# An expert stage worked in pairs of tiles, its first pair prepared inside the attention steps

## What is computed

```python
xn = layernorm(x)
x  = x + attention(xn) + ffn(xn)

def gating(t, sim, gates):                 # one weight per token and expert
    logits = normalize(t) @ normalize(sim) - sigmoid(gates)
    gated  = relu(logits)                  # experts with gated > 0 are active;
    ...                                    # a token with none gets its two best
    return softmax(masked gated)

def ffn(x):
    n1 = layernorm(x, w, b); rw = gating(n1, ...)
    q, k, v = weighted sums over 8 experts; attn = causal softmax attention
    hs = x + weighted sum over 8 experts of attn @ o_proj
    n2 = layernorm(hs, w, b); rw2 = gating(n2, moe_sim, moe_gates)
    inter = gelu(n2 @ w1[e])               # per expert e
    return hs + sum_e rw2[:, e] * (inter @ w2[e])
```

## Time and profile before

| | us |
|---|---|
| median of 3 runs | 1577.72 (1576.56 to 1579.24) |
| profiled execution | 1577.96 |
| its span, first to last instruction | 1576.2 |
| TensorE busy | 1338.6 (85%) |
| VectorE busy | 1081.8 (69%) |
| ScalarE busy | 815.0 (52%) |
| GpSimd busy | 341.4 (22%) |

### The profile page before, as it was taken

How to read it: one execution, slowest core, us unless ns; L and a number is a source line. 1 busy time by engine, 2 the same in 40 slices (tenths; PEclk the granted TensorE clock), 3 DMA queues, 4 the chain that set the end, 5 groups by cost and what they waited for, 6 DMA issues and landing times.

```text
span 1576.2 us, 34759 instructions
## 1 busy us (share of the span) xinstructions
PE 1338.6 (85%) x10534; PEld 1024.4 (65%) x10628; DVE 1081.8 (69%) x4153; ACT 815.0 (52%) x1752; POOL 341.4 (22%) x422
## 2 busy tenths in 40 slices
PE   1289999999899999999999999999994588888887
PEld 0157777777777777777777777777773355555555
DVE  7567766777777667777776777777634577777771
ACT  1136556566655566666556566665662344444342
POOL 3011221111122111111221111112111233333332
PEclk9689999999999999999999999999997699999999
DMA  4413323222233232322333322233200333223332
GB/s 108 96 45 77 79 73 100 74 78 69 68 82 76 76 99 68 79 68 72 80 75 85 89 77 70 69 79 79 75 34 10 115 135 127 102 107 134 133 135 81
DMA packets 86696, 133.21 MB, mean 85 GB/s; under 512 B 9163, under 2 KB 77115, under 8 KB 77371
## 3 DMA queue, kind: packets, MB, share of 16 engines
q1 hardware_dynamic: 86098, 132.10, 29.5%
q10 hardware_dynamic: 488, 0.01, 0.0%
HBM read 108.76 MB, written 21.50 MB: 83 GB/s over the span
## 4 chain that ended last, share of the span: by engine, by line
PE 54%; DVE 18%; ACT 11%; issue 9%; DMA 4%; DVEq 1%; SPq 1%; POOL 1%; ACTq 0%; POOLq 0%
PE ps L1363 6%; PE ps L1364 5%; PE ps L1408 5%; PE ps L1373 5%; PE ps L1572 4%; PE ps L1341 4%; PE ps L1237 3%; DMA qst<-mT 3%; PE ps L1322 3%; ACT pr L651 2%; DVE ats L1164 2%; PE ps L1299 2%; PE ps L1564 2%; PE ps L1292 2%; PE ps L1295 1%
## 5 line engine op out<-in xcount | busy, mean ns | idle before, releaser
L651 ACT ACTIVATE pr<-ps 128x512 f32<-128x512 f32 x384 | 227.2, 592 | 176.6 <-PE ps L1322 155.7
L1007 DVE TENSOR_REDUCE mx<-ps 128x2 f32<-128x512 f32 (+1 forms) x384 | 264.2, 689 | 49.8 <-PE ps L1299 26.8
L515 POOL TENSOR_TENSOR n1s<-rep,n1T 128x256 f32<-128x256 f32 x256 | 176.9, 729 | 292.5 <-PE ps L1373 274.7
L656 ACT ACTIVATE ps<-trn 128x512 f32<-128x512 bf16 x382 | 229.7, 601 | 12.1
L1572 PEld LDWEIGHTS ps<-w2s,ats 128*128 128x128 f32 x1024 | 127.3, 191 | 91.7 <-DVE ats L1164 47.8
L1572 PE MATMUL ps<-w2s,ats 128*128 128x128 f32 x1024 | 140.3, 280 | 34.2 <-DVE ats L1164 26.6
L522 POOL TENSOR_TENSOR zt<-xn,rstd 128x256 f32<-128x256 f32 x32 | 19.6, 612 | 655.2 <-DVE rstd L849 655.2
L1363 PE MATMUL ps<-n1s,wq 128*128 128x256 f32 x512 | 159.8, 394 | 0.0
L783 ACT ACTIVATE n1s<-ps 128x512 f32<-128x512 f32 x128 | 76.4, 597 | 156.5 <-PE ps L1564 155.1
L1364 PE MATMUL ps<-n1s,wk 128*128 128x256 f32 x512 | 152.7, 380 | 0.0
L1373 PE MATMUL ps<-wv,n1s 128*128 128x128 f32 x1024 | 150.6, 280 | 0.0
(11 more groups left out here) (222 smaller groups left out, 2482.2 us busy)
## 6 DMA issues: line engine op xcount, KB each, us to landing
rep<-scr_rw SPq DMA_DIRECT2D x32, 1024.0 KB, 5.1
qst<-scr_rw SPq DMA_DIRECT2D x8, 2048.0 KB, 7.5
kst<-scr_rw SPq DMA_DIRECT2D x8, 2048.0 KB, 7.5
scr_parts<-parts SPq DMA_DIRECT2D x64, 192.0 KB, 2.3
qst<-scr_parts SPq DMA_DIRECT2D x192, 64.0 KB
kst<-scr_parts SPq DMA_DIRECT2D x32, 192.0 KB
xt<-in_x SPq DMA_DIRECT2D x32, 128.0 KB, 2.3
kst<-scr_parts SPq DMA_DIRECT2D x32, 128.0 KB
```

What stands on the lines that cost most here:

```text
L515: pool.tensor_tensor(n1s[:, e], rep[:, par, e], n1T[:, par], ALU.mult).then_inc(n1s_done, 1)
L651: act.activation(pr[:, G % 2, i], ps[:, S2[k % 2]], ACT.Exp).then_inc(exp_done, 1)
L656: act.activation(ps[:, S2[k % 2]], seeds[:, 1 if (k + 2) % 3 == 2 else 0], ACT.Copy).then_inc(seed_done, 1)
L1007: dve.tensor_reduce(mx[:, min(i, 1), h:h + n], ps[:, S1[k % 2]].rearrange("p (h t) -> p h t", h=n), AX_X, ALU.max, negate=True).then_inc(s ...
```

## The change

Tiles are prepared in pairs (`NP` = 8 pairs, `BP` = 8 blocks):

- One `layer_norm2`, one `gating` and one `weights_T2` per pair, on 8 blocks at once. The gating of the next pair lies in the first tile of a pair, beside scalings 2 to 6 (`GELU_AT`), the norm of the pair after that behind it.
- The logits are formed by token: for each block of 128 tokens the normalised block itself is the stationary operand and the 8 columns of `simn` (or 2 columns of ones, for the squared norm) move. There is no copy and no transpose back.
- GpSimd does nothing in this stage. The norm is applied by ScalarE (`scale_norm2`, one instruction per block with scale and bias), all scalings are VectorE's. `n2T` has eight buffers and `hg` four (two of each before), so the copy `place_norm2` is gone, and the pipeline of up, gelu, scaling and down runs on across tiles: `up(k + 2)` follows `down(k)` for k from 0 to 127.
- The weights go to DRAM in eight pieces a pair, and come back in two halves of 1 MB a tile.
- The norm of the first pair is computed in the attention step before the last, that of the second pair, and the logits, gating and weights of the first pair, in the last one.

The diff without its removed lines and without what repeats:

```diff
+LN2_LINKS = 3 + 10
+NP = MS // 2
+BP = 2 * TM
+LG_W = 16
+GELU_AT = (5, 11, 17, 22, 28)
...
+            def store_weights2(g):
                 sp_.wait_ge(rwT2_done, g + 1)
+                for t in (2 * g, 2 * g + 1):
+                    if t >= 4:
+                        sp_.wait_ge(rep2_lo_in[t % 2], 16 * (t // 2 - 1))
+                        sp_.wait_ge(rep2_hi_in[t % 2], 16 * (t // 2 - 1))
+                    r = TM * E * (t % 2)
+                    for i in range(TM):
+                        sp_.dma_start(scr_rw2[t % 4, :, i], rwT[r + E * i:r + E * i + E, 0:P]).then_inc(rw2_stored, 16)
+            def spread2(t):
+                sp_.wait_ge(rw2_stored, 16 * 2 * TM * (t // 2 + 1))
+                for half, arrived in enumerate((rep2_lo_in, rep2_hi_in)):
+                    if t < 2:
+                        sp_.wait_ge(s2_out, UNITS * (NB - 1 + t))
+                    else:
+                        sp_.wait_ge(hgs_done, E * (t - 2) + E // 2 * (half + 1))
+                    src = scr_rw2[t % 4, E // 2 * half:E // 2 * (half + 1)].rearrange("(o e) i p -> o (e i p)", o=1)
+                    sp_.dma_start(rep2[t % 2][half].rearrange("p e t -> p (e t)"),
+                                  src.broadcast_to((P, E // 2 * W2))).then_inc(arrived[t % 2], 16)
...
+            store_weights2(0)
+            spread2(0)
             sp_.wait_ge(base_done, NB)
             store_base(NB - 1, 1)
+            spread2(1)
             sp_.wait_ge(base_stored, 16 * NB)
+            sp_.wait_ge(pv_out, NG * NB)
+            load_base(0)
+            for g in range(NP):
+                if g:
+                    store_out(2 * g - 1)
+                load_base(2 * g + 1)
+                if g + 1 < NP:
+                    store_weights2(g + 1)
+                    spread2(2 * g + 2)
+                store_out(2 * g)
+                if g + 1 < NP:
+                    load_base(2 * g + 2)
+                    spread2(2 * g + 3)
+            store_out(MS - 1)
+            for stored in out_stored:
+                sp_.wait_ge(stored, 16 * NP)
...
+            def scale_norm2(t):
+                act.wait_ge(ln2_chain, LN2_LINKS * (t // 2 + 1))
+                if t >= 2:
+                    act.wait_ge(zT2_out, t - 1)
+                else:
+                    act.wait_ge(ln_out, NB)
+                for i in range(TM):
+                    k = TM * (t % 2) + i
+                    ins = act.activation(z2[t % 2][:, i], hs[:, TM * t + i], ACT.Identity, bias=nmr[:, k:k + 1],
+                                         scale=rstd[:, t % 2, i:i + 1])
+                ins.then_inc(z2_done, 1)
+            def evac_norm2(t):
+                act.wait_ge(zT2_out, t + 1)
...
+                act.activation(n2T[t % 8], ps[:, NT_BANK(t)], ACT.Identity, bias=lnp[:, 3:4],
+                               scale=lnp[:, 2:3]).then_inc(n2T_done, 1)
+            def square2(t):
+                act.wait_ge(n2T_done, t + 1)
...
+                act.activation(sq2[t % 2], n2T[t % 8], ACT.Square).then_inc(sq2_done, 1)
...
+            def evac_weights2(g):
+                act.wait_ge(rwT2_out, g + 1)
...
+                act.activation(rwT[:, 0:P], ps[0:BP * E, WT_BANK(g), 0:P], ACT.Copy).then_inc(rwT2_done, 1)
...
+                if n_x == 0:
+                    evac_norm2(0)
+                    square2(0)
                 for k in range(3, 8):
                     exps(n, k, n_x == 0)
+                    if n_x == 0 and k == 4:
+                        evac_norm2(1)
+                        square2(1)
                     if k == 6:
                         evac_pv(n, 0)
                 exps(n, 8, n_x == 0)
+                if n_x == 0:
+                    scale_norm2(2)
+                    gate_tanh2(0)
                 exps(n, 9, n_x == 0)
...
                 evac_soft(n)
+                if n_x == 0:
+                    evac_norm2(2)
+                    square2(2)
+                    scale_norm2(3)
                 evac_pv(n, 1)
...
                 evac_att(n)
+                if n_x == 1:
+                    scale_norm2(0)
+                    scale_norm2(1)
+                if n_x == 0:
+                    evac_weights2(0)
+                    evac_norm2(3)
+                    square2(3)
...
+            def gelu(t, e):
+                k = E * t + e
+                act.wait_ge(up_out, k + 1)
+                if k >= 4:
+                    act.wait_ge(hgs_done, k - 3)
+                act.activation(hg[:, k % 4], ps[:, UP[k % 3]], ACT.Gelu).then_inc(gelu_done, 1)
+            for g in range(NP):
                 for e in range(E):
+                    gelu(2 * g, e)
+                    if e == 0 and 0 < g < NP - 1:
+                        square2(2 * g + 3)
+                    if e == 3 and g + 1 < NP:
+                        gate_tanh2(g + 1)
+                for e in range(E):
+                    gelu(2 * g + 1, e)
+                    if e == 1 and g + 1 < NP:
+                        evac_weights2(g + 1)
+                    if g + 2 < NP:
+                        if e in (3, 4):
+                            scale_norm2(2 * g + 1 + e)
+                        if e == 6:
+                            evac_norm2(2 * g + 4)
+                            square2(2 * g + 4)
+                        if e == 7:
+                            evac_norm2(2 * g + 5)
...
+            def layer_norm2(g):
+                c = Chain(dve, ln2_chain, g, LN2_LINKS)
+                dve.wait_ge(hs_done, 4 * g + 4)
+                if g:
+                    dve.wait_ge(z2_done, 2 * g)
+                else:
+                    dve.wait_ge(zp_done, NB)
+                bsf, bmf = (v[:].rearrange("p a i k -> p (a i) k") for v in (bst, bmv))
+                y, v = (w[:].rearrange("p a i -> p (a i)") for w in (rstd, vstd))
+                for i in range(BP):
+                    dve.bn_stats(bsf[:, i], hs[:, BP * g + i])
+                    if i % 2:
+                        yield
+                dve.drain()
+                for i in range(BP):
+                    ins = dve.bn_aggr(bmf[:, i], bsf[:, i])
+                    if i == TM:
+                        yield
+                c.add(ins)
+                yield
+                c.wait()
+                c.add(dve.tensor_scalar(v, bmf[:, :, 1], EPS, None, ALU.add))
+                yield
+                c.wait()
+                yield from rsqrt(dve, c, y, v, rtmp[:])
+                c.add(dve.scalar_tensor_tensor(nmr[:], bmf[:, :, 0], -1.0, y, ALU.mult, ALU.mult))
+                c.close()
...
+                norm = (layer_norm(n + 3, 1 - u) if n_x == 3 else layer_norm2(0) if n_x == 1 else
+                        layer_norm2(1) if n_x == 0 else iter(()))
...
+                    if n_x == 0:
+                        run(norm)
+                        gating(0, BP, 1, gate2, LG2(0), E, beside_gating)
+                    else:
+                        for k in range(1, GATE_LINKS + 1):
+                            beside_gating(k)
+                        run(norm)
...
+            def scale_gelu(t, e):
+                k = E * t + e
+                dve.wait_ge(gelu_done, k + 1)
+                dve.wait_ge((rep2_lo_in, rep2_hi_in)[e // (E // 2)][t % 2], 16 * (t // 2 + 1))
+                if k >= 2:
+                    dve.wait_ge(moe_out, k - 1)
+                else:
+                    dve.wait_ge(oe_out, NB)
+                dve.tensor_tensor(hgs[:, k % 2], hg[:, k % 4], rep2[t % 2][e // (E // 2)][:, e % (E // 2)], ALU.mult
+                                  ).then_inc(hgs_done, 1)
...
+            def pair(g):
+                a, b = 2 * g, 2 * g + 1
+                scale_gelu(a, 0)
+                if g:
+                    finish(a - 1)
+                scale_gelu(a, 1)
                 def beside_gating(k):
+                    if k in GELU_AT:
+                        scale_gelu(a, 2 + GELU_AT.index(k))
+                if g + 1 < NP:
+                    gating(g + 1, BP, 1, gate2, LG2(g + 1), E, beside_gating)
                 else:
+                    for k in GELU_AT:
+                        beside_gating(k)
+                norm = layer_norm2(g + 2) if g + 2 < NP else iter(())
+                for e in range(2 + len(GELU_AT), E):
+                    scale_gelu(a, e)
+                    for _ in range(4):
+                        next(norm, None)
+                for e in range(E):
+                    scale_gelu(b, e)
+                    if e == 0:
+                        finish(a)
+                    for _ in range(6):
+                        next(norm, None)
+            for g in range(NP):
+                pair(g)
+            finish(MS - 1)
...
+            def norm_T2(t):
+                pe.wait_ge(z2_done, t + 1)
...
+                for i in range(TM):
+                    ins = pe.transpose(ps[:, NT_BANK(t), i * P:(i + 1) * P], z2[t % 2][:, i], ident[:])
+                ins.then_inc(zT2_out, 1)
+            def logits2(g):
```

(57 more changed lines are left out.)

353 lines of the change are left out of this document (79 added, 274 removed).

## The result

| | before | after |
|---|---|---|
| median, us | 1578.48 (1576.56 to 1580.17, 4 runs) | 1534.1 (1530.68 to 1535.61, 4 runs) |
| ratio | | 0.9723, 95% interval 0.9704 to 0.9742 |
| profiled execution: time, span, us | 1577.96, 1576.2 | 1535.61, 1533.8 |
| end of step 30 of the attention to the first scaling, us | 76.87 | 41.15 |
| first scaling to the last sum, us | 325.54 | 318.09 |

The change makes the kernel 44.4 us faster by the medians; 1528 was forecast, within 1502 to 1555. Most of it is the hand-over: in the profiled executions 35.7 us come there and 7.5 us in the stage that follows. (End of step 30: the write of hs at 1170.33 us before and 1171.09 after; nothing ahead of it differs.)

What follows compares the result with a forecast made beforehand. Bound by a serial hand-over hole, then by TensorE at 82% busy, delayed by GpSimd's scalings. Hand-over 37 us, last two tiles 8, the rest the middle: 1577.96 - 51.4 + 1.5 = 1528 us, eight in ten within 1502 to 1555.

Steps and rivals of the forecast that it cites:

- Attention lengthened by 7.2 us: Last attention step: preparing the first pair inside it makes attention end 7.2 us later, at 1204.6 (bounds 3 and 12).
- The order's price: Last attention step: TensorE waits in order for the second square before the logits; next attention product 5.4 us later.
- First scaling 36.6 us earlier: Hand-over: first scaling of an expert's output at 1210.6 instead of 1247.20 us, 36.6 us gained.
- The trip of the weights: Hand-over: eight writes of the weights take 3.8 us, then the first 1 MB half of the spread lands after 5.1.
- The pair of 40.9 us: Middle of the expert stage: TensorE's work 32.67 us plus 8.25 of waits, 40.9 us per pair.
- the row taken for them: Logits of a pair: 32 weight loads at the profile's repeat of 0.111 us, 3.55 us (bounds 1.4 to 6.1).
- The clock at 1.00 in the stage: Expert stage: TensorE's granted clock stays at 1.00; only the restart after the hand-over was charged, +1.5 us.
- the rival of the clock: Each pair's logits and wait lower the clock: 3.5 us, seven times, 24 us in all, giving 1552; chance 13%.
- The sum: Whole kernel: last down product at 1520.1 instead of 1571.55, 51.4 us less, plus 1.5: 1528 us; 65%.
- its bounds: Whole kernel: logits -14 to +18 us and hand-over -4 to +5 around the forecast time, given as 1511 to 1548.
- Other signs: Profile: pairs repeating every 41 us; wrong if under 38 or over 44, spread waits at tile heads, attention ending after 1212.
- One sign of being wrong: Expert stage: a granted clock of TensorE below 0.95 after 1220 us would show the forecast wrong.

Runs made afterwards that it cites:

- second execution: The changed kernel, untouched, measured and profiled once more: median 1530.95 us (1528.07 to 1534.92).
- undone hand-over: Changed kernel with the first pair's preparation and the second pair's norm moved behind the last attention steps: 1548.68 us, ratio to the kernel before 0.9827.
- Moving the one cause and the other: Two runs against the changed kernel: third gelu scaled ahead of the gating, 1521.86 us; evacuation of the transposed weights one gelu later, 1520.0 us.
- the split kernel: Changed kernel with only the logits split, first tile's behind down(0) and second tile's behind down(1) of the pair: 1531.29 us (1528.93 to 1532.93).

## Why the prediction was right

**Attention lengthened by 7.2 us:** 8.4 us. The last step took 35.61 us in the profile of after, 35.54 in its second execution. The order's price, the wait of TensorE for the second square, is in the trace (0.74 us ahead of the logits at 1180.18). The rest of the difference goes with the clock, which was low for 3.4 us behind the logits. Each further 3.4 us made the step 1.6 us longer (35.5, 37.2 and 38.8 us above), so with the clock at 1.00 it would have taken some 33.9 us by my estimate, 6.7 more than before. The forecast left the clock at 1.00 in the attention.

**First scaling 36.6 us earlier:** 35.7 us, measured from the end of step 30. The trip of the weights was put at 3.8 us and 5.1 us; it is 3.60 (1203.88 to 1207.48) and 4.76 (to the first scaling at 1212.24). The undone hand-over confirms that doing it inside is worth 22 of these. What the forecast did not separate: 13.6 us come from the rewritten preparation alone.

**The pair of 40.9 us:** close, and partly by luck. It was forecast with the clock at 1.00, and the full pairs with the shortest low stretch are 40.60 us; without its 0.8 us they would be 39.8 (the estimate above), so the waits were put some 1.1 us too high in all. The parts that can be compared hold: 1.85 us were forecast behind the logits and 1.79 measured, behind the weight transpose 1.8 and 1.57 us (of TensorE's idle time), and for the logits 3.55 and 3.5 us (their products start 3.38 us apart, first to last, at full clock). Moving the one cause and the other took 1.8 us off the third pair (40.89 to 39.10, of which 0.8 is the fall that was missing) and 1.7 us off the shortest (40.60 to 38.91), so both waits were real. The scaling of the norms, four in 1.65 us where the forecast had four of 0.4, took the time it was given.

The logits at full clock start every 0.111 us, the row taken for them; with the 107 ns of a load and the floor of 25 ns for a small product of the Trainium skill (TensorE: Matmul & The Clock Gate, sections "LDWEIGHTS (loading the stationary operand)" and "Back-to-back issue gap"), added up, they would start every 132 ns. The trace does not agree with adding them.

**The clock at 1.00 in the stage:** wrong. This is the step that failed, and the rival of the clock came true in its mechanism and not in its price. That rival put it at 3.5 us in each of seven pairs, as if every product behind it were late by its own lengthening; by the pairs and the estimate above it is 0.8 us (low for 3.4 us) to 3.2 us (low for 10.2), because VectorE sets the pace in most of the stretch where the clock is low, and TensorE's slower products fill part of its waits. Over pairs two to seven that is 10.2 us in after and 7.1 in its second execution. It shows up in the logits, whose products start 3.38 us apart, first to last, at full clock and up to 4.40 us apart where it falls within them; in the first pair, 44.36 us from the first scaling to its second sum where the split kernel has 42.13; and in the seventh, 38.19 us where the split kernel, in which it does not fall there, has 36.65. In sum the stage of after is 8.4 us longer than the one with the logits split, and the pairs separate it: where both are low for 3.4 us they are equally long, so the split gains by where and how long the clock is low, and nothing else of it shows. The forecast for the stage was 13.3 us under before (51.4 less the hand-over's 36.6, and 1.5 for the restart); after has 7.5 and, in its second execution, 10.3, the split kernel 15.8. So the forecast came this near because two errors stood against each other, waits put too high and a clock put too high, besides a first pair that started slowly: its logits ended 11.4 us behind the first scaling, where the forecast had 7.8 and 1.5 for the clock. The Trainium skill (TensorE: Matmul & The Clock Gate, section "HAM oscillation — how this bites in real kernels") has kernels whose gap in each round throttles every round anew; the traces agree in the pattern, seven falls in seven pairs, and here the wait was 1.79 us, behind loads, and in five of the pairs the clock fell ahead of it.

**The sum:** the profiled execution took 1535.6 us and not 1528. Of the 7.6 us 0.8 came ahead of the change (1171.09 against 1170.33), 0.9 is the hand-over, and 5.9 the stage. The second time the profiled execution of the same kernel took 1528.1 us, by an attention that ended 4.5 us earlier and a stage in which the clock fell as often but stayed low for less (three of seven times 3.4 us, and never 10.2). So the forecast is the fast end of the kernel's own spread. Two of its figures are off without touching it: its bounds, added up, give 1510 to 1551 and not 1511 to 1548, and the last two tiles of before take 32.5 us by their final sums (1540.20 to 1572.74) and not 34.6, so that 4.9 us were gained there and not 8 (27.61 in after).

**Other signs:** VectorE kept the pace it was given (no full pair under 40.58 us in after), the weights never held up a middle tile (the spreads land in 6.9 us, not 5.1, and yet no wait for a DMA stands at the head of one), and the last attention step did not stretch by 10 us. One sign of being wrong came true, the granted clock below 0.95 after 1220 us (0.91 over 1300 to 1480). The chain is bound as described: what shortened the kernel was what shortened a wait for VectorE's scalings.

The landing of the spreads, from the page's list of transfers (count, KB each, median us from issue to landing):

```profile
qst<-scr_rw SPq DMA_DIRECT2D x16, 1024.0 KB, 6.9
```

## What to carry to other kernels

When a serial preparation stands between two stages, the gain is in the hand-over: price every instruction of it that moves inside the earlier stage, then look at what that stage's in-order engines must wait for. A wait put down to the engine that delivers (VectorE here) may belong to another one's queue (ScalarE, blocked by a small evacuation placed one gelu too early): moving that one line gave 11 to 14 us, more than the whole change gave in the stage (7.5 and 10.3 us). And before a rewrite is credited, its simplest part should be timed alone; here moving the scalings off GpSimd by itself shortened the stage by 18.5 us, more than the whole change did.
